# Layer 0's attention loop: two low parts computed in other slots, first value products that wait for plain blocks only, and the last output product between the weight transpositions

## The reference, cut to what matters

```python
x = x + tanh(g_xattn[0]) * L0_xattn(layernorm(x), ctx, mask, ...)   # 32 heads of width 128
x = x + tanh(g_ffn[0])   * L0_ffn(layernorm(x), ...)                # 4-bit codes, looked up in a table
# L0_xattn: q = rmsnorm(h) @ w_q.T ; k = ctx @ w_k.T ; v = ctx @ w_v.T
#           score = q.k + position_bias, masked softmax ; attn = score.v ; out = h + attn @ w_out.T
# then layer 1: the same two steps with other weights and 8 key/value heads
```

## Time and profile before

| what | value |
|---|---|
| time, 3 runs | median 1716.46 us (1714.38 to 1718.55) |
| the profiled execution | 1714.45 us, of which its span is 1712.6 us |
| TensorE matmul busy | 1671.6 us (98%), 10269 instructions |
| VectorE, ScalarE, GpSimd busy | 1193.6, 1001.6, 589.2 us |
| granted TensorE clock, mean | 0.997 of full speed |

### The profile page before, as it was taken

How to read it: one execution, slowest core, us unless ns; L and a number is a source line. 1 busy time by engine, 2 the same in 40 slices (tenths; PEclk the granted TensorE clock), 3 DMA queues, 4 the chain that set the end, 5 groups by cost and what they waited for, 6 DMA issues and landing times.

```text
span 1712.6 us, 30969 instructions
## 1 busy us (share of the span) xinstructions
PE 1671.6 (98%) x10269; PEld 1483.0 (87%) x10269; DVE 1193.6 (70%) x2245; ACT 1001.6 (58%) x2540; POOL 589.2 (34%) x584
## 2 busy tenths in 40 slices
PE   8999999999889999999999999999999999999998
PEld 7999999999788888888887788888888888888886
DVE  6444446576687777877778876768676777777676
ACT  5344434345766767667676566665666656666563
POOL 2322223210324343343435433333333333333343
PEclk9999999999999999999999999999999999999999
DMA  6444433544323333333323010101011111111001
GB/s 221 174 147 165 153 147 147 190 161 156 101 73 107 111 110 101 119 99 113 107 85 128 23 61 16 58 25 61 22 51 34 49 37 46 37 37 40 13 7 50
DMA packets 80592, 153.31 MB, mean 90 GB/s; under 512 B 6545, under 2 KB 58129, under 8 KB 76945
## 3 DMA queue, kind: packets, MB, share of 16 engines
q1 hardware_dynamic: 80528, 152.50, 26.5%
HBM read 108.43 MB, written 44.04 MB: 89 GB/s over the span
## 4 chain that ended last, share of the span: by engine, by line
PE 83%; DVE 9%; ACT 4%; issue 2%; DMA 1%; POOL 1%; SPq 0%; DVEq 0%; ACTq 0%; POOLq 0%
PE bank L2046 21%; PE bank L1993 14%; PE bank L1995 14%; PE bank L1994 14%; PE bank L2222 6%; PE bank L2438 3%; PE bank L2257 2%; PE bank L2180 2%; PE bank L2339 2%; PE bank L2464 2%; PE bank L2168 1%; DVE qw_lo L1322 1%; DVE nmax L1543 1%; DVE sc L1541 1%; PE bank L2469 1%
## 5 line engine op out<-in xcount | busy, mean ns | idle before, releaser
L1993 PE MATMUL bank<-w_hi,xt_hi 128*128 (+2 forms) x512 | 178.0, 348 | 0.8 <-DVE qt_lo L1900 0.8
L748 POOL TENSOR_TENSOR p<-p,rn 128x512 f32<-128x512 f32 x128 | 133.1, 1041 | 122.7 <-DVE rn L1872 119.5
L691 POOL TENSOR_TENSOR pr<-pr,rn 128x512 f32<-128x512 f32 x64 | 66.6, 1041 | 313.5 <-DVE rn L1558 313.5
L1995 PE MATMUL bank<-w_hi,xt_lo 128*128 (+2 forms) x512 | 172.6, 337 | 0.0
L1994 PE MATMUL bank<-w_lo,xt_hi 128*128 (+2 forms) x512 | 171.3, 335 | 0.0
L1199 ACT ACTIVATE p<-bank,nb,q_r 128x256 f32<-128x256 f32 x256 | 141.0, 561 | 5.0 <-DVE nb L1867 2.6
L610 POOL TENSOR_TENSOR q_r<-q_ms,half 128x4 f32<-128x4 f32 x64 | 64.4, 1007 | 192.1 <-DVE q_ms L1846 192.1
L1047 ACT ACTIVATE pr<-sc,nmax 128x128 f32<-128x128 f32 x256 | 99.8, 391 | 48.9 <-DVE nmax L1543 48.5
L1993 PE MATMUL bank<-w0o_hi,ot_hi 128*128 128x512 f32 x256 | 106.0, 414 | 14.7 <-DVE residual L1550 12.5
L1993 PE MATMUL bank<-w_hi,ot_hi 128*128 (+1 forms) x256 | 106.1, 415 | 1.9 <-DVE ot_lo L1888 1.9
L610 POOL TENSOR_TENSOR k_r<-k_ms,half 128x2 f32<-128x2 f32 x64 | 56.8, 888 | 147.6 <-DVE k_ms L1825 147.6
(11 more groups left out here) (294 smaller groups left out, 5539.4 us busy)
## 6 DMA issues: line engine op xcount, KB each, us to landing
stage<-w SPq DMA_DIRECT2D x35, 512.0 KB, 3.3
keys_of_layer<-kout SPq DMA_DIRECT2D x16, 1024.0 KB, 4.5
values_of_layer<-vout SPq DMA_DIRECT2D x16, 1024.0 KB, 5.2
kt<-keys_of_layer SPq DMA_DIRECT2D x64, 256.0 KB, 3.2
vs<-values_of_layer SPq DMA_DIRECT2D x64, 256.0 KB, 2.8
vraw<-wv SPq DMA_DIRECT2D x10, 1024.0 KB, 6.7
kraw<-wk SPq DMA_DIRECT2D x16, 512.0 KB, 5.6
stage0o<-w SPq DMA_DIRECT2D x16, 512.0 KB, 4.2
```

What stands on the lines that cost most here:

```text
L691: pool.tensor_tensor(by4(pr), by4(pr), rn[:, :].unsqueeze(2).to_broadcast([P, 4, P]), ALU.mult).then_inc(norm_done, 1)
L748: pool.tensor_tensor(p1[:, half_p:half_p + 2, :], p1[:, half_p:half_p + 2, :], rn1[:, half_p:half_p + 2].unsqueeze(2).to_broadcast([P, 2, ...
L1993: nc.tensor.matmul(out_ap, l_hi, r_hi, start=(c == 0), stop=False)
L1995: op = nc.tensor.matmul(out_ap, l_lo, r_hi, start=False, stop=(c == n - 1))
```

## The change

Six edits, on all five engines:
- **GpSimd, start:** the first sums of the values' weight wait for `ksum_done` 4 (the sums of the keys' weight) and no more for `kw_lo_done` 4.
- **ScalarE, start:** the rounding of the values' sums comes ahead of `part2(0, 2)`. **TensorE:** products 1 and 2 of job 3 wait for `vw_lo_done` 2 (plain blocks), products 6, 7, 5 for 3.
- **VectorE, loop:** `query_weight_early_lo` moves from the end of slot p = 1 to slot p = 2 behind `accumulate`; `output_weight_lo` moves from the end of slot p = 3 to the following slot p = 1, ahead of `dequantise`.
- **SyncE, loop:** the load of stage0o moves from slot p = 0 to slot p = 1, behind `load_values`.
- **End of the loop:** `row_stats(1, 0)` moves behind `output_lo(U - 1)` on VectorE. TensorE does the last projection between pieces 1 and 2 of `transpose_weight`. ScalarE's last `output_hi` and the transposed rows 0, 1 come ahead of the normalised rows 2, 3, and `first_rounded(0)` comes behind the four roundings of the weight.

```diff
@@ -510,14 +510,14 @@
                 if isinstance(t, int) and t == 0 and j == 1:
                     sp.wait_ge(w_lo_done[0], 2)
                     load_weight(0, 2)
-                if p == 0 and not (isinstance(t, int) and t == 0 and j == 0) and not (last and j >= 4):
-                    sp.wait_ge(w_lo_done[1], n + 1)
-                    sp.dma_start(stage0[1][:, :], w0[1:, 1, :, :][n]).then_inc(w_in[1], 16)
                 if p == 3 and not last:
                     sp.wait_ge(bm_done, 4 * (n + 1))
                     sp.dma_start(bias_sb[:, parity, :], bias0[n + 2, :, :]).then_inc(bias_in[parity], 16)
                 if not (isinstance(t, int) and t == 0 and j == 0) and not (last and j == 7):
                     load_values(t + (j + 1) // BODY, (j + 1) % BODY)
+                if p == 1 and not (isinstance(t, int) and t == 0 and j == 1) and not (last and j >= 4):
+                    sp.wait_ge(w_lo_done[1], n + 1)
+                    sp.dma_start(stage0[1][:, :], w0[1:, 1, :, :][n]).then_inc(w_in[1], 16)
 
             for j in range(BODY):
                 slot(0, j)
@@ -650,7 +650,7 @@
                 if not last:
                     weight_sums(kraw, kraw_in, ksum_done, 2 * s + 2, 2 * s + 1)
 
-            pool.wait_ge(kw_lo_done, 4)
+            pool.wait_ge(ksum_done, 4)
             weight_sums(vraw, vraw_in, vsum_done, 0, 0)
             weight_sums(kraw, kraw_in, ksum_done, 2, 1)
             weight_sums(vraw, vraw_in, vsum_done, 1, 1)
@@ -913,10 +913,10 @@
                     quarter12(s, 1)
                     part2(s, 2)
                 else:
-                    part2(s, 2)
                     act.wait_ge(vsum_done, 4)
                     act.wait_ge(product_done, 8)
                     nc.scalar.activation(vw_hi[:, S2:S4 + 1, :, :], vraw[:, S2:S4 + 1, :, :], ACT.Copy).then_inc(vw_hi_done, 1)
+                    part2(s, 2)
                 part4(s, 2)
                 part1(s, 3)
                 quarter12(s, 2)
@@ -1135,14 +1135,14 @@
             probabilities_copied(U)
             normed_rows(1, 0)
             normed_rows(1, 1)
-            first_rounded(0)
-            normed_rows(1, 2)
-            normed_rows(1, 3)
             output_hi(U, BODY - 1)
             transposed_hi(1, 0)
             transposed_hi(1, 1)
+            normed_rows(1, 2)
+            normed_rows(1, 3)
             for c in range(C):
                 weight_hi(c)
+            first_rounded(0)
             normed_rows(1, 4)
             normed_rows(1, 5)
             transposed_hi(1, 2)
@@ -1640,9 +1640,6 @@
                     dequantise(n, p, i + 1)
                     inverse_sums(i + 1, 2 * p)
                     accumulate(i - 1, 2 * ((j - 2) % 4))
-                    if j == BODY - 1:
-                        dve.wait_ge(acc_done, U - 3)
-                        row_stats(1, 0)
                     return
                 if first and j == 0:
                     dve.wait_ge(kd_out, 16 * NG + 32 * EG)
@@ -1654,6 +1651,8 @@
                     if first and j < 3 + B // 2:
                         dve.wait_ge(base_done, 2 * (j - 3) + 2)
                     accumulate(i - 2, 2 * ((j - 3) % 4))
+                if p == 2 and not last and not (first and j == 2):
+                    query_weight_early_lo(n + 2)
                 if first and j == 0:
                     residual_factors()
                     dve.wait_ge(valid_done, 1)
@@ -1681,11 +1680,9 @@
                     quarter11_of_queries(n + 1, 1 - parity)
                 if active and p == 2:
                     quarter22_of_queries(n + 1, 1 - parity)
+                if p == 1 and not (first and j == 1):
+                    output_weight_lo(n, parity)
                 dequantise(n, p, i + 1)
-                if p == 1 and not last and not (first and j == 1):
-                    query_weight_early_lo(n + 2)
-                if p == 3 and not last:
-                    output_weight_lo(n + 1, 1 - parity)
 
             for j in range(BODY):
                 slot(0, j)
@@ -1728,6 +1725,8 @@
                 feed_forward(1, gate_lo[:, b:b + 1], b)
 
             output_lo(U - 1, (BODY - 2) % 2)
+            dve.wait_ge(acc_done, U - 3)
+            row_stats(1, 0)
             dve.wait_ge(acc_done, U - 2)
             row_stats(1, 1)
             dve.wait_ge(fbias_in, 16)
@@ -2091,7 +2090,8 @@
             def weight_ready(s, k, part):
 
                 if of_values(k):
-                    pe.wait_ge(vw_lo_done, 3 if isinstance(s, int) and (s, k) == (0, 3) else 3 * group_of(s, k) + part)
+                    first_strassen = isinstance(s, int) and (s, k) == (0, 3)
+                    pe.wait_ge(vw_lo_done, min(part + 1, 3) if first_strassen else 3 * group_of(s, k) + part)
                 elif part < 3:
                     pe.wait_ge(kw_lo_done, number(s, k) + part)
 
@@ -2355,9 +2355,11 @@
             transpose_rows(1, 1)
             pe.wait_ge(wl_done, C * 2 ** LO_BITS + 1)
             pe.wait_ge(added, U)
-            for c in range(C):
-                transpose_weight(c)
+            transpose_weight(0)
+            transpose_weight(1)
             output_projection(U, BODY - 1, NG - 1)
+            transpose_weight(2)
+            transpose_weight(3)
             transpose_rows(1, 2)
             transpose_rows(1, 3)
             pe.wait_ge(fw_lo_done, C)
```

## The result

The changed kernel takes **1707.28 us** (median of four executions, 1706.29 to 1708.21); the kernel before took 1715.42 beside it (1713.92 to 1718.55). The ratio is 0.995, 95% interval 0.9933 to 0.9967: 8.1 us faster by the medians, where 6.7 were forecast. The profiled execution took 1707.12 us with a span of 1705.3, 7.3 less than the 1712.6 of before.

A forecast was written before the change was run, and what follows sets the result against it. The prediction took TensorE, busy for 98% of the span, as the bound, with only its idle and slow stretches to win back. Savings of 3.0 + 1.0 + 1.2 + 1.5 = 6.7 off 1716.46 gave 1709.8 us, range 1704.5 to 1714.3.

The forecast's parts named there:

- The forecast case: Whole kernel: the four savings come about as summed, giving 1707 to 1712 us; chance 0.62.
- start: Kernel start: the 5.00 us wait goes, about 3.0 come at product 5; 3.0 us saved, bounds 0.7 and 6.1.
- loop's first iteration: Loop's first iteration: moved low parts shorten one wait by 1.65 and lengthen a later one; net 1.0, bounds 0 and 1.7.
- hardware loop: Slots 1 and 2 of each pair: maxima start 0.10 us earlier, twelve times; 1.2 us saved, at most 3.4.
- end of the loop: Behind the loop: projection 1.74 us earlier, low_ffn about 1.5 earlier; bounds 0.8 and 2.4.
- the clock's 1.6: Start: 1.6 us taken off the 4.6 saved, for a clock fall behind the new wait of 3.0.
- the alternation of whole operations: Where VectorE and GpSimd meet: each waits for the other's operation under way; used for start and hardware loop.
- the start's wait only moves: Rival, start: part2 is kept back as long as TensorE idled before, start saves 0.7; 1712.1 us, chance 0.13.
- the engines don't hold each other up: Rival, VectorE and GpSimd: start gives 6.1, hardware loop 3.4, 12.0 in all; 1704.5 us, chance 0.13.
- w0o_lo pushes the maxima: Rival, hardware loop: TensorE's wait grows by 1.0 in each of twelve slots; slower, 1723 us, chance 0.05.
- nothing in the loop: Rival: the loop's edits gain nothing, first iteration included, and the start only moves; 2.2 saved, 1714.3 us, chance 0.07.

The follow-up runs named there:

- e1: Only the change's edits at the start (GpSimd's wait, ScalarE's order, TensorE's waits), on the kernel before: ratio 0.9981 to it, 3.3 us less.
- e12: The kernel before once more, unchanged, one execution with its trace; no time of its own is given.
- e4: The changed kernel with ScalarE's part2(0, 2) put back ahead of the rounding of the values' sums: ratio 0.9940 to the kernel before.
- e3: Only the edits behind the loop (row_stats(1, 0), ScalarE's order, the last projection between transpositions), on the kernel before: ratio 0.9988 to it, 2.1 us less.
- e2: Only the edits in the loop's slots (SyncE's load, w0o_lo, qw_lo), on the kernel before: ratio 0.9980 to it, 3.4 us less.
- e8: The changed kernel with layer 1's third statistics, row_stats(1, 2), moved behind the low parts of the weight: ratio 0.9954 to the kernel before.
- e11: The changed kernel once more, unchanged: 1708.62 us.
- e7: The changed kernel with GpSimd's sums of the query weight made one slot later: ratio 0.9925 to the kernel before.

## Why the prediction was right, step by step

The forecast case came: 1707.28 lies just inside its own range of 1707 to 1712. Its four terms against the shifts of the two profiled executions:

| term | forecast | measured |
|---|---|---|
| start | 3.0 | 4.4 |
| loop's first iteration | 1.0 | 2.0 |
| hardware loop | 1.2 | 1.8 |
| end of the loop | 1.5 | 0.6 |
| layer 1 | 0 | -1.4 |
| sum | 6.7 | 7.4 |

That the sums agree so well is in part luck: 1.0 too much in the first iteration is a long wait of one execution, 1.4 too much at the start and 1.4 lost in layer 1 are falls of the clock that came elsewhere than I had them, and the end gave 0.9 less.

- **Start: the mechanism and its times were right; the clock's 1.6 was a toss-up.** Forecast were GpSimd's last sum at 35.5, VectorE's subtraction until 31.6, product 5 at 38.0 behind 3.0 us; measured 35.55, 31.68, 38.12 and 2.90. So the alternation of whole operations, taken from one meeting at 460, held for operations of other sizes. The gain was 4.4 against 4.6 with the clock kept. It did stay at 1.00 in this execution, fell behind the same wait in e1, and fell elsewhere in the changed kernel. The Trainium skill, page "TensorE: Matmul & The Clock Gate", Part 1, says of a kernel's first, slow products that their number varies from run to run; e12 shows the like 41 us into the span, with 0.67 against 0.50 in the same stretch behind the same wait. Over all traces the term was about right: the first attention product comes at 433.7 on average in the four with the old start, at 429.7 in the four with the new start and no fall, and at 430.9 in the two with a fall. That is 4.0 and 2.8 where I had 4.6 and 3.0. In the changed kernel's profiled execution the fall that I had taken off came elsewhere: it appears in the table as layer 1's -1.4.
- **The rival "the start's wait only moves"** is out by the 4.4 and by e1, whose 3.3 (1.7 to 4.8) leaves no room for 0.7. In a weaker sense it holds one step on: of the 2.9 that e4 took from the new wait, 1.5 were lost again by the first attention product, 1.18 of it as the wait at 53.76.
- **First iteration: the mechanism and the 1.0 were right; the 2.0 of the table are not all the edits'.** In the kernel before's profiled execution TensorE waited 2.28 us for `queries_of_layer`, where three other traces with the same order show 1.19 to 1.21:

```profile
437.48 1.16 PE L2257 MATMUL bank<-kt,queries_of_layer 128*128 128x128 f32 x8 [2.28 <-ACT queries_of_layer L980]
```

TensorE's waits in the first iteration, and the time from the first attention product to the end of the wait for qt_t_lo:

| trace | low parts | queries_of_layer | three accumulation waits | in all |
|---|---|---|---|---|
| before | old places | 2.28 | 2.84, 1.73, 1.24 | 67.95 |
| e12 | old | 1.21 | 2.83, 1.48, 1.25 | 66.93 |
| e3 | old | 1.19 | 2.83, 1.49, 1.24 | 66.91 |
| e1 | old | 1.19 | 2.83, 1.55, 1.25 | 66.85 |
| e2 | new | 1.19 | 2.83, none, 1.78 | 65.83 |
| changed | new | 1.45 | 1.73, 0.93, 1.78 | 65.94 |

e2 against e1, e3 and e12 parts order and clock, since in all four the clock fell once in this stretch, behind the 2.83. The middle wait goes, as I had it (1.65 to come off one of 1.73), the third grows by 0.54, which was my figure, and 1.0 to 1.1 are left of the forecast 1.0. In the changed kernel the fall came earlier, at 432. The three traces with a fall there (changed, e8, e11) have 1.7 for the first wait and 0.93 for the middle one; in the eleven others the first is 2.8.
- **Hardware loop: right mechanism, 0.10 was a little small.** The wait fell from 0.46 to 0.30: 0.16 a pair. I had w0o_lo at about 1.4 (1.47 measured) and GpSimd's first query sum 0.59 behind it (0.58). wl ended at 633.32, 1.13 behind w0o_lo's end, where I had 1.20: that is the 0.06 by which the gain was larger. The rival "the engines don't hold each other up" is out by 1.21 against 0.74 in e7; "w0o_lo pushes the maxima" by the wait that shrank; "nothing in the loop" by twelve times 0.16. The Trainium skill, page "GPSIMD Engine Reference", section Key points, gives the contention for VectorE instructions with two inputs in on-chip memory; the two-input w0o_lo and wl agree (1.22 to 1.47, 0.75 to 1.21).
- **End: this is the step that failed.** The projection behind the loop came 9.9 - 8.2 = 1.7 earlier, as forecast (1.74). But then I had "its rounding and low part (0.6 + 0.7 us) hold TensorE for about 0.7", and it was 1.61. On VectorE `row_stats(1, 2)` stands ahead of the low parts, and the two-column `base_b` in it took 1.22 in place of 0.17 beside GpSimd's bias additions of 1.26 each. I had counted statistics by their size, and `first_rounded(0)` as hidden by just these additions, without asking what the additions do to VectorE. e3 shows the same 1.21 and 1.59 alone. e8 moves the whole of these statistics away and gets 0.17 and 0.70, which shows that they held the low parts. That the stretched `base_b` alone makes the 0.9 is read from rows and not tested by itself: without its extra 1.05 the low parts would have been ready as soon as in e8, where the last one ends at 922.67, behind ScalarE's w_hi (until 921.84 there, 921.67 in the changed kernel). e8 does not show what the 0.9 were worth, since its own order made the new wait of 0.94. In the changed kernel they were not made up later: the shift is 8.8 at `low_ffn` and still 8.8 at the next long wait (976.33 and 967.53).

By e3's timing the end is worth 2.1 (0.5 to 3.6), by the trace 0.6. From the last projection of a slot p = 2 to `low_ffn` the old end took 76.6 us in the two traces where the clock stayed up (before, e2) and 77.6 and 77.7 in those where it fell behind the 1.9 for ot_lo (e12, e1); the new end took 75.9 to 76.0 in the changed kernel and in e3. So the edit is worth 0.6 or 1.7, by whether the clock would have fallen, which the forecast of 1.5 did not ask; e3's executions ran from 0.994 to 0.998 of the clock, so its timing can't say how often.

## What to carry to other kernels

Between kernels whose waits differ by a few microseconds, compare the granted clock of many executions, and the same wait in several traces, before a shift is put down to an edit: here 2.4 to 3.1 of 8.3 us go with the clock, partly at waits that no edit touched, and 1.0 us of a shift of 2.0 was one long wait of a single execution. Before an operation of VectorE is moved next to GpSimd's, or the other way, look in the trace whether operations of these forms hold each other up, and if they do, count that each waits for the whole operation of the other that is under way, even where it is tiny itself; the free place is behind the operations that TensorE waits for. And when a wait is removed, look for what feeds the next one: e4's 2.9 us shrank to 1.4, e8's 0.9 to nothing.

## What the runs showed of the hardware that was not expected

- A VectorE operation on 128x2 elements took 1.22 us (0.17 alone) beside GpSimd's additions of 128x512, which take 1.26 each: the price is set by the other engine's operation, not by its own size. Not every operation pays it: beside the same additions of the changed kernel (915.90 to 920.93) two of the statistics' first step took 1.28 together, as they did at 911.15 with GpSimd idle, and ot_lo and an accumulation, which read a bank, 0.69 and 0.75, their usual times. Those shown stretched here are the subtractions whose operands both lie outside the banks (kw_lo, w0o_lo, qw_lo), wl, and this one.
- The same kernel had its TensorE clock at half speed in other stretches from one execution to the next: before, 10.2 and 13.7 us in two traces; changed, 6.8 and 6.8 but at 432 and 968 in one and 432 and 496 in the other. In the changed kernel's first trace a wait of 1.45 us was followed by a fall, and those of 2.90 and 2.78 were not; in the kernel before the same wait was of 2.28 us and was not followed by one. (Time at half clock is summed here over windows of 5 us, as twice what is missing from 1.00.)
- A fall costs less than its lost cycles, on average. 0.001 of the mean clock is 1.7 us of full speed over this span, and the time moved by 1.1 us (45 executions of before) to 1.4 us (e3's eleven); over all 122 executions of the twelve kernels with more than one, each about the mean of those run beside it, it is 1.1. The clock is on record in steps of 0.001, and by an estimate from its spread of 0.001 this alone flattens the line by some 8%, too little to make up the difference. An explanation is that while TensorE is slow, the engines that it would wait for next catch up. One place fits it: with the fall behind the first accumulation wait (e2) the middle wait is gone, and with the fall at 432 (changed) it is 0.93. The Trainium skill, page "TensorE: Matmul & The Clock Gate", section Terms, puts the penalty at the throttled time times the share of the clock withheld, by which 0.001 would be the full 1.7 us; the kernel before paid 65% of it and e3 82%.
